# Weight pieces of the first expert loop: three output slots, loads two ahead, issued by POOL instead of SP

## The reference

```python
# block 0: 256 -> 512 -> 256, gated
h = einsum('nd,ehd->neh', xf, w1); g = einsum('nd,ehd->neh', xf, w3)
out = einsum('ned,ne->nd', einsum('neh,edh->ned', silu(h) * g, w2), comb)
# block 1: 256 -> 1024 -> 256
h = silu(xf @ w1[i] + b1[i]); y = h @ w2[i] + b2[i]; out = out + y * comb[:, i:i+1]
```

## Time and profile before

| | |
|---|---|
| median of 3 runs | 1355.62 us (1351.83 to 1357.24) |
| the profiled execution | 1357.27 us, span 1355.5 us |
| granted TensorE clock, mean over the span | 0.819 of full speed |
| PE busy in the span | 959.7 us (71%) |
| DVE, ACT, POOL busy | 838.5, 562.7, 418.1 us |
| DMA: queue 1 (SP) and queue 0 (POOL) | 35.6% and 8.9% of 16 engines |

### The profile page before, as it was taken

One profiled execution on the slowest core, in us unless ns is written; L12 is line 12 of the kernel. 1 busy time (PEld: TensorE's weight loads), 2 busy tenths in 40 slices (PEclk: granted clock), 3 DMA queues, 4 the chain that ended last, 5 costly groups with the idle time before them and its releaser, 6 DMA issues.

```text
span 1355.5 us, 26742 instructions
## 1 busy us (share of the span) xinstructions
PE 959.7 (71%) x7185; PEld 785.9 (58%) x7185; DVE 838.5 (62%) x1909; ACT 562.7 (42%) x1227; POOL 418.1 (31%) x478
## 2 busy tenths in 40 slices
PE   5210386746798887888881088755999999999953
PEld 4100265614676666676661067614888888888842
DVE  6999489897644445445444966593555555555545
ACT  5255323356564454455442013373433443344312
POOL 1385000000144445445442050003443444344410
PEclk8655695557799999999996596556999999999975
DMA  7066105905555655655566701203343442442257
GB/s 249 1 209 209 54 0 173 315 8 154 181 166 168 200 175 173 195 175 177 178 183 213 264 0 46 78 0 86 110 152 87 136 136 77 140 134 75 75 162 251
DMA packets 189007, 188.66 MB, mean 139 GB/s; under 512 B 91232, under 2 KB 158248, under 8 KB 188840
## 3 DMA queue, kind: packets, MB, share of 16 engines
q1 hardware_dynamic: 170616, 145.19, 35.6%
q0 software_dynamic: 14000, 38.82, 8.9%
q10 hardware_dynamic: 4352, 4.20, 0.9%
HBM read 119.46 MB, written 49.28 MB: 124 GB/s over the span
## 4 chain that ended last, share of the span: by engine, by line
PE 39%; DMA 16%; issue 16%; DVE 11%; ACT 6%; SPq 5%; DVEq 2%; POOL 2%; ACTq 1%; POOLq 1%
PE bank L711 15%; PE bank L733 14%; DMA wreg<-in_L_ffn_w_dram 7%; PE bank L644 4%; DMA region<-rows_x,fetch_now 3%; SPq L347 2%; DMA split_v<-wreg 2%; PE bank L561 2%; DMA wreg<-rows_y 2%; ACT xt L883 2%; PE bank L616 1%; ACT wreg L833 1%; POOL rows_y L505 1%; DVE st_lg L996 1%; PE bank L769 1%
## 5 line engine op out<-in xcount | busy, mean ns | idle before, releaser
L711 PE MATMUL bank<-xt,wreg 128*128 x3360 | 384.4, 275 | 20.1 <-DMA xt<-region 17.6
L711 PEld LDWEIGHTS bank<-xt,wreg 128*128 128x128 f16 x3360 | 328.0, 99 | 70.5 <-issue 29.1
L733 PE MATMUL bank<-wreg,region 128*128 128x256 f16 x2520 | 297.9, 276 | 51.3 <-ACT region L912 48.2
L733 PEld LDWEIGHTS bank<-wreg,region 128*128 128x128 f16 x2520 | 239.3, 99 | 103.2 <-ACT region L912 64.0
L505 POOL DMA_INDIRECT rows_y<-region,put_now x140 | 154.6, 1104 | 273.3 <-DVE region L1362 126.4
L917 ACT ACTIVATE region<-bank,b_t,wreg 128x256 f32<-128x256 f32 x280 | 142.1, 561 | 226.7 <-PE bank L711 225.7
L463 POOL DMA_INDIRECT region<-rows_x,fetch_now x144 | 142.9, 993 | 160.5 <-issue 108.2
L1298 DVE SCALAR_TENSOR_TENSOR wreg<-wreg x70 | 49.6, 750 | 181.1 <-ACT wreg L893 178.9
L1354 DVE TENSOR_SCALAR region<-region,wreg 128x512 f16<-128x512 f32 x140 | 76.2, 544 | 73.3 <-ACT region L917 72.8
L561 PE MATMUL bank<-ident,xn 128*128 128x128 f32 x256 | 54.2, 371 | 83.3 <-DVE xn L1005 77.1
L1357 DVE SCALAR_TENSOR_TENSOR region<-region,wreg 128x512 f16<-128x512 f32 x140 | 106.1, 758 | 5.0
(11 more groups left out here) (238 smaller groups left out, 1168.9 us busy)
## 6 DMA issues: line engine op xcount, KB each, us to landing
wreg<-in_L_ffn_w_dram SPq DMA_DIRECT2D x136, 256.0 KB, 3.0
wreg<-in_L_ffn_w_dram SPq DMA_DIRECT2D x48, 512.0 KB, 6.1
split_v<-wreg SPq DMA_DIRECT2D x35, 512.0 KB
wreg<-split_v SPq DMA_DIRECT2D x32, 512.0 KB
wreg<-rows_y SPq DMA_DIRECT2D x48, 256.0 KB, 3.5
rows_x<-region SPq DMA_DIRECT2D x16, 512.0 KB, 3.3
wreg<-in_x_dram SPq DMA_DIRECT2D x4, 1024.0 KB, 9.5
out_dram<-xt ACTq DMA_DIRECT2D x16, 256.0 KB, 3.3
```

Source lines behind the costliest of these rows:

```text
L711: last = pe.matmul(to, block, x_cols[:, bass.ds(b, 1), :, xs_, k, :].rearrange("p j r n -> p (j r) n"), start=(k == 0 and ws_ + xs_ == 0), ...
L733: last = pe.matmul(yb[:, r * C:(r + 1) * C], lhs[:, c, r * P:(r + 1) * P], block, start=first, stop=end, skip_group_check=True)
```

## The change

The pieces are loaded and stored by POOL instead of SP, `piece_out` has three slots (n % 3), and the loads run two pieces ahead of the tile. SP's loop of the first mixture keeps only the transposes. POOL waits before its loop until all weights of block 0 have been transposed, loads piece 0, waits for it, and loads piece 1. In round n, after the put of tile n, it waits for three things in loops of one round, each followed by an increment of a semaphore that nobody waits for: store n - 1 landed, piece n + 1 landed, low halves of piece n written. Then it stores piece n and loads piece n + 2. ACT's wait for the stores is removed. After its loop POOL also waits for the last loads. `load_half` for `v1_rows` and `v2_rows`, `load_piece` and `store_piece` move from the sync block to the gpsimd block with `sp` turned into `pool`.

```diff
-        piece_out = wreg[:, 26624:28672]... (j=2, m=2, s=2)
+        piece_out = wreg[:, 26624:29696]... (j=3, m=2, s=2)
...
 def turn_tiles(f):            # SP
-                if f == 0:
-                    sp.wait_ge(w_turned, 6 * E)
-                    load_piece(0)
                 for e in range(E):
                     with sp.Fori(edges[e], edges[e + 1]) as n:
                         sp.wait_ge(z_ready[f], 4 * n + 4)
                         turn_rows(f, n + 2)
-                        if f == 0:
-                            with sp.Fori(n, n + 1) as m:
-                                sp.wait_ge(piece_loaded, 32 * m + 32)
-                            load_piece(n + 1)
-                            split = sp.snap(n + 1)
-                            sp.wait_ge(piece_lo, split)
-                            store_piece(n)
...
 def feed_experts(f):          # POOL
                 fetch_next(0)
+                if f == 0:
+                    pool.wait_ge(w_turned, 6 * E)
+                    load_piece(0)
+                    pool.wait_ge(piece_loaded, 32)
+                    load_piece(1)
                 with pool.Fori(0, total) as n:
                     fetch_next(n + 1)
                     put(n)
+                    if f == 0:
+                        for waited, each, more in ((piece_stored, 16, 0), (piece_loaded, 32, 64), (piece_lo, 1, 1)):
+                            with pool.Fori(n, n + 1) as m:
+                                pool.wait_ge(waited, each * m + more)
+                                pool.sem_inc(pieces_passed, 1)
+                        store_piece(n)
+                        load_piece(n + 2)
...
 def split_hi(n):              # ACT
                 with act.Fori(n, n + 1) as m:
                     act.wait_ge(piece_loaded, 32 * m + 32)
-                with act.Fori(n, n + 1) as m:
-                    act.wait_ge(piece_stored, 16 * m)
                 for m in range(2):
-                    act.activation(piece_out[:, bass.ds(n % 2, 1), m, 0]...
+                    act.activation(piece_out[:, bass.ds(n % 3, 1), m, 0]...
```

More of the change, by code:

```diff
@@ L107, in bass_metaformer @@
         piece_in = wreg[:, 24576:26624].rearrange("p (j m n) -> p j m n", j=2, m=2)
-        piece_out = wreg[:, 26624:28672].bitcast(F16).rearrange("p (j m s n) -> p j m s n", j=2, m=2, s=2)
+        piece_out = wreg[:, 26624:29696].bitcast(F16).rearrange("p (j m s n) -> p j m s n", j=3, m=2, s=2)
         sum_in = wreg[:, 30720:32256].rearrange("p (j n) -> p j n", j=3)
@@ L264, in bass_metaformer @@
         sum_loaded, summed, peak1_ready = [sem(f"sum_loaded{j}") for j in range(3)], sem("summed"), sem("peak1_ready")
-        v_loaded = sem2("v_loaded")
+        v_loaded, pieces_passed = sem2("v_loaded"), sem("pieces_passed")
         stage_loaded = sem2("stage_loaded")
@@ L305, in load_half @@
                 return sp.dma_start(to.rearrange("p (c d) -> p c d", c=2), v2_rows[bass.ds(n, 1)].rearrange("a p c d -> p (a c) d"))
+            v1_rows, v2_rows = v1.rearrange("e (k p) f -> (e k) p f", p=P), v2.rearrange("e (q c p) d -> (e q) p c d", c=2, p=P)
             def store_rows(f, i):
@@ L347, in turn_rows @@
                     sp.dma_start_transpose(to, x_rows[:, r]).then_inc(xc_ready[r][f], 16)
[L349 to L358, removed]
             def load_v(e):
@@ L392, in _ @@
             total = turn_tiles(0)
-            for waited, each, more in ((piece_loaded, 32, 32), (piece_stored, 16, 0), (xc_ready[0][0], 16, 32),
+            for waited, each, more in ((piece_stored, 16, 0), (xc_ready[0][0], 16, 32),
                                        (xc_ready[1][0], 16, 32), (y_free[0], 32, 16)):
@@ L475, in spread_peaks, with load_half, load_piece, store_piece @@
                                                P, bass.bass_isa.ReduceOp.max).then_inc(peak_spread[f], 1)
+            v1_rows, v2_rows = v1.rearrange("e (k p) f -> (e k) p f", p=P), v2.rearrange("e (q c p) d -> (e q) p c d", c=2, p=P)
+            def load_half(to, m, n):
+                if m == 0:
+                    return pool.dma_start(to, v1_rows[bass.ds(n // 2, 1), :, bass.ds(n % 2 * 512, 512)].rearrange("a p f -> p (a f)"))
+                return pool.dma_start(to.rearrange("p (c d) -> p c d", c=2), v2_rows[bass.ds(n, 1)].rearrange("a p c d -> p (a c) d"))
+            def load_piece(n):
+                slot, piece = (n, n) if isinstance(n, int) else (n % 2, n % PIECES)
+                for m in range(2):
+                    load_half(piece_in[:, bass.ds(slot, 1), m].rearrange("p j n -> p (j n)"), m, piece).then_inc(piece_loaded, 16)
+            def store_piece(n):
+                pool.dma_start(split_v[bass.ds(n % PIECES // 4, 1), :, bass.ds(n % 4 * (2 * FH[1]), 2 * FH[1])].rearrange("a p n -> p (a n)"),
+                             piece_out[:, bass.ds(n % 3, 1)].rearrange("p j m s n -> p (j m s n)")).then_inc(piece_stored, 16)
             def feed_experts(f):
@@ L527, in all_done @@
                     pool.wait_ge(y_free[f], 32 * m + 48)
+                    if f == 0:
+                        pool.wait_ge(piece_loaded, 32 * m + 96)
                 after(total - 1, all_done)
@@ L1296, in split_lo @@
                 for m in range(2):
-                    hi, lo = (piece_out[:, bass.ds(n % 2, 1), m, s_].rearrange("p j n -> p (j n)") for s_ in range(2))
+                    hi, lo = (piece_out[:, bass.ds(n % 3, 1), m, s_].rearrange("p j n -> p (j n)") for s_ in range(2))
                     last = dve.scalar_tensor_tensor(lo, piece_in[:, bass.ds(n % 2, 1), m].rearrange("p j n -> p (j n)"),
```

3 lines of the change are left out of this document (1 added, 2 removed).

## The result

The changed kernel takes 1348.27 us (median of 11 runs, 1344.07 to 1351.21), the kernel before 1355.33 us beside it (11 runs). The ratio is 0.9941, with a 95% interval of 0.9922 to 0.9960: 7 us or 0.6% faster, in the forecast direction and inside the forecast range of 1318 to 1378, but less than half of the 16.6 us that were forecast.

A forecast was written before the change was run, and what follows sets the result against it. A ring through ACT's wait for the store bounds the first expert loop at 10.19 us a tile; POOL's loop would then take 9.65. 34 x (10.19 - 9.65) = 18.4 us off 1357.27 gives 1339; eight in ten, 1318 to 1378.

The forecast's parts named there:

- What bounds the kernel: First expert loop: a ring of ACT's split, y's copy, puts, fetches, SP's transposes and store sets 10.19 us a tile.
- POOL's price: First expert loop: three waits and three DMAs added to POOL's 7.6 us round make 9.2 to 10.0; 9.65 taken.
- The engine's count: POOL engine, first put to fetch_now's copy: puts, gap and three plain DMAs sum to 4.1 to 5.2 us.
- the count of the queue: POOL's queue, first put to fetch_now's copy: issues, waits and register work sum to 4.3 to 5.0 us.
- Rival A: The forecast itself: POOL sets the first loop's pace at 9.2 to 10.0 us a tile; chance 0.50.
- C: First loop: gain used up, POOL at 10.0 to 10.4 us, one ring for another, 1351 to 1364 us; chance 0.18.
- The sum: First loop: 34 periods x (10.19 - 9.65) = 18.4 us off the profiled 1357.27 gives 1338.9; 1339 kept.
- a put beside split_lo: First loop: POOL's put beside DVE's split_lo takes 1.50 us, its twin 0.98; they exclude each other for 0.5.
- D: Slower: register-addressed plain DMA costs POOL 1.0 and 0.30 gap; loop 11.0, 1384 us; decides from 0.87 each; chance 0.16.
- E: Slower: DVE shuts out POOL's plain DMAs too; one 0.5 us stretch gives 10.15, two 10.65, 1373 us; chance 0.10.
- Part 1: First loop: ACT's wait for the store goes; that alone would bring a tile to 8.7 us, the gain's ceiling.
- SP never binds: First loop: SP loses two loads and a store a tile and keeps the transposes alone, so it never binds.

The follow-up runs named there:

- experiment 9: Against experiment 1, loads one ahead and ahead of the store, all issued by SP, three slots kept; 1342.78 us, ratio 0.9899 to the kernel before.
- experiment 3: Changed kernel plus one unused plain 256 KB load a round on POOL, with its wait; 1378.55 us, ratio 1.0171 to the kernel before.
- experiment 5: Piece transfers cut to an eighth of their bytes: against experiment 1 (SP issuing) 1289.89 us, against the changed kernel (POOL issuing) 1348.68 us.
- experiment 1: Changed kernel with a piece's loads, store and waits issued by SP behind the transposes, three slots and loads two ahead kept; 1332.68 us, ratio 0.9844.
- experiment 7: Against experiment 1, the store alone cut to 64 KB, loads whole; 1300.31 us, ratio 0.9576 to the kernel before.
- experiment 2: Changed kernel with two output slots and ACT's wait for the stores back, issue still on POOL; 1348.51 us, ratio 0.9935 to the kernel before.
- experiment 6: Against experiment 1, the store moved to POOL, loads left on SP, three slots; 1308.29 us, ratio 0.9643 to the kernel before.
- experiment 10: Against experiment 6, two output slots and ACT's wait for the store; four runs of 1349.6 to 1381.9 us, the fastest 0.993 of the kernel before.
- experiment 8: Changed kernel with the store issued by SP, the two loads left on POOL, three slots; 1329.16 us, ratio 0.9779 to the kernel before.

## Why the prediction was right and wrong

**What bounds the kernel: right.** The ring through ACT's wait, POOL's puts and fetches, SP's transposes and the store was there: experiment 9 cuts it at ACT's wait alone and gains 13 to 14 us, and in the changed kernel the wait of 104.6 us vanished as forecast.

**POOL's price: right where it is undisturbed, to the hundredth by luck.** The working gave 9.2 to 10.0, and 9.65 was picked in it. A plain DMA 0.59, 0.57 and 0.71 us (forecast 0.62, 0.62, 0.62 to 1.24); the copy of fetch_now 4.82 us after the first put (4.4 to 5.2); 0.90 us before the first put; 9.66 us in all (9.65). Experiments 3 and 5 show that this sum, with its lengthenings, sets the changed kernel. The engine's count had no gaps between the plain DMAs; there are 0.13, 0.46 and 0.10 us, which the count of the queue had in effect. Rival A's mechanism held, but the mean round of 10.00 us stands on its border with C, "the gain is used up".

**The sum: here it failed.** "34 periods x (10.19 - 9.65)" used one price for all 34 rounds, that of a round in which nothing goes wrong, while the 10.19 it was taken from is a mean over rounds. The term that was mis-sized is POOL's mean round, 10.00 us: 9.66 and 0.34, of which some 0.23 (7.9 / 34) are POOL's indexed DMAs and copies lengthened by DVE and 0.14 two long issues. The text had the first in hand: a put beside split_lo takes 1.50 us "in nearly every tile", and it went into the range and not into the 9.65. The 1.50 us put itself mostly did not return (puts lost 1.0 us in the whole loop); the fetches and the copies met split_lo instead. On a loop with 0.54 us to gain, 0.34 us is over half. 34 x 0.34 = 11.6 us less gain, 2.2 back at the start and 0.8 more at the end make 10.2 us; the profiled run took 1349.04 us against a sum of 1338.9.

**The long issues: not foreseen, though the trace of before had one.** It stands in the last section. POOL had slack there (the next put, at 650.57, still waits 1.25 us for ACT), but the fetch behind the pause was late, and that round and the three after it take 10.64, 12.86, 8.68 and 10.96 us, 2.4 more than four mean ones. Whether the late fetch did that is not shown.

**Rivals D and E: both fall.** No plain DMA took POOL 1.0 us and 0.30 behind it: the three take 2.56 us with their gaps (517.42 to 519.98), 0.85 each, where D had 1.30. That is just under D's limit of 0.87, which was taken from a round with a put of 1.50 us; the undisturbed round without the three is 0.5 us shorter than the 7.6 of the prediction. And none of the 104 in the loop was lengthened by DVE (0.71 us beside split_lo at 539.01).

**Part 1, "That alone would bring a tile to ... 8.7 us": wrong.** The slot alone brings it to 9.68 us (experiment 9), with the loads two ahead to 9.24 (experiment 1): ACT then waits for the load, and behind that the ring of fetch and transposes binds. As a ceiling for PE, 8.7 was too high: it can go at 8.2 us a tile (experiment 5).

**"SP never binds", told of the changed kernel: true, and the wrong comparison.** The prediction weighed what POOL pays, and never what the same slot and order would bring with SP left as issuer. SP's time did not have to be relieved (experiment 7): 1332.7 us with SP, 1348.3 with POOL. Part 1 also gave the credit for the broken ring to the third slot. In the changed kernel it has none (experiment 2): there, POOL issues the store early enough and is itself later than ACT. On SP it is worth 13 us, and in the best version some 39, with the weaker wait not tried.

## What to carry to other kernels

Price the engine that is to take over the issue as a whole round, and take a mean for it, with the lengthenings that its neighbours cause, if you subtract it from a mean: a margin of half a microsecond goes in single disturbed rounds. What the parts of a change are worth is known only once they are run one by one: here the slot and the earlier load gave 23 us, the move to POOL took some 15 of them back, and one of the three transfers moved alone (the store) gave 24 more. And a buffer that shows no gain behind one bound can be worth most of the gain once that bound is gone.

## What the runs showed of the hardware

**A long issue on POOL's queue at a fixed place in its program.** In the changed kernel the 101st, 196th, 294th and 368th DMA of POOL's 399 comes after a pause of its queue of 2.6 to 3.2 us with nothing to wait for, in the kernel before the 114th and the 259th of 290. The version with small pieces has the same four places though its data differ, and the pause before the fetch has the same length (its timeline of POOL, and that of the kernel before at its 113th DMA, where a fetch elsewhere comes after 1.25 us):

```profile
504.06 1.04 POOL L442 DMA_INDIRECT region<-rows_x,fetch_now  x1 [3.55 <-issue]
```

```profile
646.83 1.01 POOL L463 DMA_INDIRECT region<-rows_x,fetch_now  x1 [3.93 <-issue]
```

Two versions that share another POOL program (experiments 6 and 10) share their places too, 114, 224 and 294, while their rounds are 8.7 and 10.5 us: it goes with POOL's instructions and not with time or traffic. One falls into the first loop of the kernel before, two into that of the changed one. The cause is open.

**Beside a DVE instruction with two SBUF inputs, POOL's small copies suffer most in proportion.** A copy of 128 x 2 values goes from 0.20 to 0.75 us, an indexed DMA from 1.03 to 1.52, a plain one not at all.

**One MB issued at once beside a fetch lengthens it.** 4.43 and 5.00 us to land in place of 2.8, in a ring that has no buffer to hide it; the same bytes with the store issued elsewhere let the whole core move 204 GB/s in place of 191.

**What a plain DMA costs POOL depends on how many stand together.** Each takes 0.57 to 0.71 us of the engine. POOL's undisturbed round is 7.66 us with the store alone (experiment 6), 8.5 with the two loads (experiment 8), 9.66 with all three, and 10.59 with one more load (experiment 3). The store adds 1.2 us to the round with the loads, though it takes 0.59: with three, the copy no longer follows without gaps, and 0.69 us of gaps stand between them in which the profile shows no wait.
